# Attention and GRU on one core: four score banks shared with other stages, and a new order of every engine's turn

## The reference

```python
scale, shift = split(cond @ W_emb + b_emb)
xn = rms_norm(x, g_norm) * (1 + scale) + shift
q, k, v = heads(xn @ W_qkv)                  # q, k: rms_norm per head, times g_q, g_k
attn = softmax(q @ k^T * 16 ** -0.5)         # 32 x 32 per head
o = attn @ v
x = x + (o + o @ W_out)

gi = x_t @ W_ih + b_ih;  gh = h @ W_hh + b_hh         # for each of 32 time steps
r, z = sigmoid(i_r + h_r), sigmoid(i_z + h_z)
n = tanh(i_n + r * h_n)
h = (1 - z) * n + z * h                               # h starts as cond
out = x + all h
```

## Time and profile before

| what | us |
|---|---|
| median of three runs | 350.33 |
| the profiled execution | 349.93 |
| its span, from the first to the last instruction | 348.1 |
| PE busy (share of the span) | 331.1 (95%) |
| DVE busy | 246.8 (71%) |
| ACT busy | 237.1 (68%) |
| POOL busy | 224.5 (64%) |
| first input product of the first GRU step (L1233) | at 199.84 |

### The profile page before, as it was taken

How to read it: one execution, slowest core, us unless ns; L and a number is a source line. 1 busy time by engine, 2 the same in 40 slices (tenths; PEclk the granted TensorE clock), 3 DMA queues, 4 the chain that set the end, 5 groups by cost and what they waited for, 6 DMA issues and landing times.

```text
span 348.1 us, 14145 instructions
## 1 busy us (share of the span) xinstructions
PE 331.1 (95%) x5201; PEld 300.5 (86%) x5201; DVE 246.8 (71%) x664; ACT 237.1 (68%) x722; POOL 224.5 (64%) x404
## 2 busy tenths in 40 slices
PE   8989999999999999999998999999999999999994
PEld 8767888878788887878877899999999999999994
DVE  1779988898989889898889555555556555555555
ACT  4788777777777777777755756666666666666663
POOL 6788776676867677686858455555555555555552
PEclk9999999999999999999999999999999999999999
DMA  6961133622111211111111131111111121111111
GB/s 203 312 208 44 30 99 106 189 80 59 58 28 50 62 46 56 29 55 60 54 36 63 39 101 47 57 52 61 59 47 60 60 60 60 60 60 60 60 53 39
DMA packets 26576, 25.81 MB, mean 74 GB/s; under 512 B 3750, under 2 KB 25260, under 8 KB 26540
## 3 DMA queue, kind: packets, MB, share of 16 engines
q1 hardware_dynamic: 24828, 22.10, 20.7%
q10 hardware_dynamic: 1712, 3.21, 3.0%
HBM read 12.46 MB, written 8.39 MB: 60 GB/s over the span
## 4 chain that ended last, share of the span: by engine, by line
PE 87%; POOL 5%; issue 4%; DVE 2%; ACT 1%; POOLq 0%; ACTq 0%; DVEq 0%
PE bank L1233 37%; PE bank L1190 23%; PE bank L1353 8%; PE bank L1334 5%; PE bank L1370 5%; PE bank L1482 2%; PE bank L1317 2%; PE bank L1326 2%; PE bank L1196 2%; POOL wqkv_lo L554 1%; POOL oT_lo L502 1%; POOL xn L476 1%; POOL operands L465 1%; PE bank L1210 1%; POOL wih_lo L495 1%
## 5 line engine op out<-in xcount | busy, mean ns | idle before, releaser
L1233 PE MATMUL bank<-wih_lo,wo_parts 128*128 128x256 f32 x192 | 56.3, 294 | 0.0
L1233 PE MATMUL bank<-wih_hi,wo_parts 128*128 128x256 f32 x192 | 54.5, 285 | 0.2 <-POOL pair_lo L580 0.2
L1233 PE MATMUL bank<-wih_hi,pair_lo 128*128 128x256 f32 x192 | 52.7, 279 | 0.0
L1233 PE MATMUL bank<-wqkv_hi,hT_hi 128*128 128x256 f32 x192 | 52.6, 293 | 0.0
L591 POOL TENSOR_TENSOR operands<-operands,h 128x128 f32<-128x128 f32 x64 | 29.6, 462 | 34.0 <-ACT operands L880 33.2
L1233 PE MATMUL bank<-wqkv_lo,hT_hi 128*128 128x256 f32 x192 | 50.0, 279 | 0.0
L1190 PE MATMUL bank<-wqkv_hi,xn_hi 128*128 128x512 f32 (+1 forms) x124 | 46.5, 375 | 0.2 <-POOL xn_lo L511 0.2
L1133 DVE TENSOR_TENSOR operands<-bank,operands 128x128 f32<-128x128 f32 x64 | 18.6, 291 | 39.4 <-ACT operands L877 39.4
L1233 PE MATMUL bank<-wqkv_hi,hT_lo 128*128 128x256 f32 x192 | 42.7, 279 | 0.0
L598 POOL TENSOR_TENSOR w_emb_sb<-h,w_emb_sb 128x256 f32<-128x256 f32 x31 | 22.9, 737 | 30.7 <-DVE h L1150 30.7
L1190 PE MATMUL bank<-wqkv_lo,xn_hi 128*128 128x512 f32 (+1 forms) x124 | 41.9, 338 | 0.0
(11 more groups left out here) (137 smaller groups left out, 991.8 us busy)
## 6 DMA issues: line engine op xcount, KB each, us to landing
v_diag<-v_rows SPq DMA_DIRECT2D x128, 34.0 KB, 1.9
out_dram<-x SPq DMA_DIRECT2D x16, 256.0 KB, 2.2
w_emb_sb<-out_dram SPq DMA_DIRECT2D x32, 128.0 KB, 2.1
out_dram<-w_emb_sb SPq DMA_DIRECT2D x31, 128.0 KB, 1.7
x_in<-in_x_dram SPq DMA_DIRECT2D x7, 512.0 KB, 9.2
stage_w<-in_L_cond_W_ih_dram ACTq DMA_DIRECT2D x2, 384.0 KB, 3.4
w_hh_sb<-in_L_cond_W_hh_dram ACTq DMA_DIRECT2D x2, 384.0 KB, 3.4
w_emb_sb<-in_L_cond_W_emb_dram ACTq DMA_DIRECT2D x1, 512.0 KB, 4.3
```

Of the source, the lines that this page charges most:

```text
L1233: return pe.matmul(dst, moved, gate_columns(weights, k, block), start=False, stop=True, skip_group_check=True)
```

## The change

**Scores.** All 32 matmuls of a group follow one another without `s_half`; the four partition groups of the operands write to four banks, 0 to 3, of which each uses the first 128 columns. The head order of scores, maxima and PV follows.

**Other users of these banks.** PV goes to bank 0 from column 128, the input transposes to the right half of bank 2, OUT to the right half of bank 3. The new bank 4 has the result transposes and V, bank 5 QKT, banks 6 and 7 QK as before. Steps that share a bank now wait for each other: the scores for the last readers of PV, of input transposes and of OUT (`o_ready`, `xmod_ready`, `x2_ready`, the last for the OUT of the turn before), the input transposes and OUT for `logits_ready`, that is, until DVE has read the scores of the same turn, and the maxima for the PV of the same turn.

**Orders.** On PE the result transposes and V move from the turn's start to behind QKT (V only from turn 11 on; `early`). DVE takes the maxima and `logits` right behind `qkn`, and then `ss`, reciprocal, `o_sb`, residual, `xmod`, `probsT`, `oT`; from turn 34 on `qkn`, maxima, `logits`, `ss`, reciprocal, `o_sb`, `oT`, `probsT`, and last the residual. ACT begins with the copies of QKT and V, then the roots. POOL begins with the masked keys, then Newton, then shift. `LATE_RESULTS`, by which four result transposes and copies came at the end of a turn, is gone.

**Gate weights.** W_ih and W_hh lie side by side in `gate_stage` and are split in sixteen pieces (128 x 2 x 96 each), one in each looped turn: a cast on ACT, a subtraction on POOL. Their loads and those of the biases are issued by SP in turns 7 to 12 instead of by ACT in turns 11 to 15, and the bias sum is in turn 14 instead of 37. W_hh no longer takes W_qkv's place. The GRU's small tiles lie in `gate_stage`, the state products of the first step come in turns 39 and 41.

```diff
-PE_X2T, PE_V, PE_S, PE_PV, PE_QKT, PE_OUT, PE_XT, PE_QK = 11, 4, 7, 8, 5, 10, 2, 3
-DVE_QKN, DVE_SS, DVE_OT, DVE_MAX, DVE_RCP, DVE_XMOD, DVE_RES, DVE_O, DVE_PT = 4, 3, 8, 6, 7, 1, 9, 7, 6
+DVE_QKN, DVE_MAX, DVE_SS, DVE_RCP, DVE_RES, DVE_XMOD, DVE_PT, DVE_OT = 4, 6, 3, 7, 9, 1, 6, 7
-GATE_LOADS = 11
-LATE_RESULTS = range(24, 28)
-LAST_TURNS = range(34, 39)
+LAST_TURNS = NG + 2
...
-        p_xTw, p_vx2, p_qkT = (bank(f"bank{i}") for i in range(3))
-        p_s = ctx.enter_context(nc.psum_tensor("bank3", [P, 2 * BANK], F32))
-        p_o = bank("bank5")
+        p_s = ctx.enter_context(nc.psum_tensor("bank0", [P, 4 * BANK], F32))
+        p_vx2, p_qkT = bank("bank4"), bank("bank5")
+        p_o = p_s[:, P:P + GB * HEADS // 4 * VW]
+        p_xT = p_s[:, 2 * BANK + D:3 * BANK]
+        p_w = p_s[:, 3 * BANK + D:4 * BANK]
...
+            def gate_piece(n):
+                lo, whole, hi = (w[:, :, :].rearrange("p m (n f) -> p m n f", n=GATE_PIECES)[:, :, n, :]
+                                 for w in (gate_lo, gate_stage, gate_hi))
+                pool.wait_ge(gate_hi_ready, n + 1)
+                pool.tensor_tensor(lo, whole, hi.bitcast(F32), ALU.subtract).then_inc(gate_lo_ready, 1)
...
             def maxima(g, slot):
                 dve.wait_ge(s_ps, g + 1)
+                if later(g, 1):
+                    dve.wait_ge(o_ps, g)
...
@@ DVE body
+                last = isinstance(base, int) and base + u >= LAST_TURNS
...
+                if last and g is not None:
+                    probs_transposed(g, (u - DVE_PT) % 2)
...
                 o = group(base, u, DVE_RES)
                 if o is not None:
                     residual(o, (u - DVE_RES) % 4)
...
@@ input_transposes
+                if later(g, PE_S - PE_XT):
+                    pe.wait_ge(logits_ready, g - (PE_S - PE_XT - 1))
...
@@ scores
+                if later(g, 2):
+                    pe.wait_ge(o_ready, g - 1)
+                pe.wait_ge(xmod_ready, capped(g, PE_S - PE_XT))
+                if later(g, PE_OUT - PE_S + 1):
+                    pe.wait_ge(x2_ready, g - (PE_OUT - PE_S))
-                for n in range(2):
-                    if n == 1:
-                        pe.wait_ge(s_half, g + 1)
...
+                for c in range(KC):
+                    for b in range(GB):
+                        columns = slice(c * P + T * b, c * P + T * b + T)
+                        for j in range(NB):
+                            rows = slice(PB * j, PB * j + PB)
+                            dst = p_s[T * b:T * b + T, BANK * j + 2 * T * c:BANK * j + 2 * T * c + 2 * T]
...
@@ output_projection
-                pe.wait_ge(xmod_ready, capped(g, PE_OUT - PE_XT))
+                pe.wait_ge(logits_ready, capped(g, PE_OUT - PE_S + 1))
```

More of the change, by code:

```diff
@@ L411, in body @@
                     load_x(4 * FIRST_SPREAD, NG, x_loaded[FIRST_SPREAD])
+                for i in range(4):
+                    if turn_is(base, u, BIAS_LOADS + i // 2):
+                        load_bias(i)
+                    if turn_is(base, u, GATE_LOADS + i):
+                        load_gate_weights(i)
                 o = group(base, u, SP_X2)
@@ L526, in body @@
             def body(base, u):
+                k = group(base, u, POOL_KEYS)
+                if k is not None:
+                    mask_keys(k, (u - POOL_KEYS) % 2)
+                n = norm_item(base, u, POOL_NEWTON)
+                if n is not None:
+                    newton(n, (u - POOL_NEWTON) % 2)
                 g = group(base, u, POOL_XN)
@@ L540, in body @@
                     input_low_part(g, (u - POOL_XLO) % 2)
[L541 to L544, removed]
+                if turn_is(base, u, BIAS_SUM):
                     summed_biases()
[L546 to L555, removed]
+                if not isinstance(base, int):
+                    gate_piece(base + (u - FIRST_LOOPED))
             pool.memset(threes[:, :], 3.0).then_inc(threes_ready, 1)
@@ L664, in value_weights, with gate_piece @@
                 act.copy(wqkv_hi[:, :, 2 * D:3 * D], stage_w[:, :, 2 * D:3 * D]).then_inc(wv_hi_ready, 1)
[L666 to L691, removed]
+            def gate_piece(n):
+                hi, whole = (w[:, :, :].rearrange("p m (n f) -> p m n f", n=GATE_PIECES)[:, :, n, :]
+                             for w in (gate_hi, gate_stage))
+                act.copy(hi, whole).then_inc(gate_hi_ready, 1)
             def first_state():
@@ L794, in body @@
             def body(base, u):
+                if turn_is(base, u, FIRST_LOOPED - 1):
+                    for loaded in ih_loaded + hh_loaded:
+                        act.wait_ge(loaded, 16)
+                if turn_is(base, u, SET_GATES):
+                    act.wait_ge(bias_ready, 1)
+                    act.wait_ge(gates_clear[0], 1)
+                    set_gates(0)
+                g = group(base, u, ACT_QKT)
+                if g is not None:
+                    queries_keys(g, (u - ACT_QKT) % 2)
+                v = group(base, u, ACT_V)
+                if v is not None:
+                    values(v, (u - ACT_V) % 4)
                 n = norm_item(base, u, ACT_LN)
@@ L808, in body @@
                 d = group(base, u, ACT_X2T)
[L809 to L810 removed]
+                if d is not None:
                     result(d)
[L812 to L814 removed]
                 g = group(base, u, ACT_EXP)
@@ L817, in body @@
                     exponentials(g, (u - ACT_EXP) % 2)
-                for c in range(KC):
-                    if turn_is(base, u, NG + c):
-                        gate_weights(c)
+                if not isinstance(base, int):
+                    gate_piece(base + (u - FIRST_LOOPED))
                 n = group(base, u, ACT_SQX)
@@ L843, in body @@
                     second_squares()
-                for i in range(2 * KC):
-                    if turn_is(base, u, GATE_LOADS + i):
-                        load_gate_weights(i)
                 if turn_is(base, u, ACT_XN):
@@ L1088, in body @@
                     last_low_part((u - DVE_OT) % 2)
-                o = group(base, u, DVE_O)
-                if o is not None and not late_residual:
-                    attention_output(o, (u - DVE_O) % 2)
+                g = group(base, u, DVE_XMOD)
+                if g is not None:
+                    modulated(g, (u - DVE_XMOD) % 2)
                 g = group(base, u, DVE_PT)
-                if g is not None and not late_residual:
+                if g is not None and not last:
                     probs_transposed(g, (u - DVE_PT) % 2)
+                o = group(base, u, DVE_OT)
+                if o is not None and not last:
+                    attention_transposed(o, (u - DVE_OT) % 2)
                 if turn_is(base, u, 0):
@@ L1321, in result_transposes @@
                 pe.wait_ge(x2_ready, d + 1)
-                pe.wait_ge(v_ready, capped(d, PE_X2T - PE_V + (1 if isinstance(d, int) and d in LATE_RESULTS else 0)))
+                pe.wait_ge(v_ready, capped(d, PE_X2T - PE_V))
                 if later(d, 1):
@@ L1411, in body @@
                     query_key_transposes(g, (u - PE_QKT) % 2)
+                d = group(base, u, PE_X2T)
+                if d is not None:
+                    result_transposes(d, (u - PE_X2T) % 4)
+                if v is not None and not early:
+                    value_projection(v, (u - PE_V) % 2)
                 if turn_is(base, u, NG - 1 + PE_OUT):
```

173 lines of the change are left out of this document (69 added, 104 removed).

## The result

The changed kernel takes 368.19 us (median of four runs, 366.7 to 369.05) against 350.42 for the kernel before on the same chip: ratio 1.050, 95% interval 1.046 to 1.054. The forecast was 353.3, range 347.0 to 356.3. The sign was right and the size was not.

A forecast was written before the change was run, and what follows sets the result against it. PE was taken to set the pace, DVE 9% behind. Start +2.55, loop -6.3, tail +7.0 and GRU 0 summed to +3.2 on the profiled 349.93 us, giving 353.1 to 353.5; forecast 353.3, range 347.0 to 356.3.

The forecast's parts named there:

- The scores, 0.57: PE's merged 32 score matmuls take 0.57 us from their start to PV, where the two halves took 1.08.
- back to back: Rival for the scores: halves merely follow without the idle 0.24 and its restart, 0.64 us to PV, 355.5 us; chance 0.2.
- the sixteen tiles' 0.37: Rival: the array takes both score halves in the time of one, 0.37 us to PV, 347.5 us in all; chance 0.19.
- The new waits in the loop: Looped turns: maxima wait for PV and OUT for `logits`, a cycle of 5.27 us; -6.3 us over 23 turns.
- The start: Turns up to the fifth scores: +2.55 us, of which +1.55 from the first to the fifth scores through added waits.
- The +1.0 ahead of group 0: Before the first scores: POOL does masked keys ahead of the shift, so the input's low part comes later; +1.0 us.
- The tail: Scores of group 27 to the first GRU product: scores wait for DVE's residual, 35.4 against 28.43 us, +7.0.
- the clock to a rival: Rival: PE's holes in the tail halve its clock, some 5 us more, 358 us in all; chance 0.05.
- The pieces and the loads: Gate-weight pieces on ACT and POOL cost nothing in the loop; earlier weight and bias loads on SP's queue are hidden.
- The GRU: GRU steps behind the tail: same instructions with other names and banks, 0 us, both signs excluded.
- Merging gains nothing: Rival: scores stay 1.08 us because the four groups' matmuls follow at the old rate; +16, about 369 us; chance 0.03.

The follow-up runs named there:

- e1: Changed kernel with every score matmul of 64 columns cut into two of 32 columns, 64 matmuls instead of 32: 415.28 us, ratio 1.185.
- e10: Changed kernel with its 32 score matmuls of 64 columns issued twice over to the same places: 415.94 us, ratio 1.186.
- e2: Changed kernel with score matmuls reordered, the four column groups changing before the row groups: 369.05 us, ratio 1.053.
- e5: Changed kernel with two of a group's six QK products moved ahead of OUT from turn 11 on: 363.94 us, ratio 1.038.
- e6: Changed kernel with V behind QKT from turn 7 on instead of turn 11: 366.41 us, ratio 1.043.
- e3: Changed kernel with matmuls that nobody reads filling PE's idle times in turns 34 to 38: 365.49 us, ratio 1.042.
- e4: Kernel before with the gate-weight part of the change alone; banks, orders and scores untouched: 349.68 us, ratio 0.997.
- e9: Changed kernel, two QK products ahead of OUT, V late from turn 7; in the tail earlier residual, unread matmuls, OUT in bank 4: 359.49 us, ratio 1.025.

## Why the prediction was wrong

- **The scores, 0.57: this is the step that failed.** They took 0.82 on the mean. The price of 6.7 ns a record came from four records in 0.27 us, which are the first four of PV's 32 where the window of the rows ends; all 32 last 0.68. The rows of the halves said otherwise as well: 0.45 and 0.39 for 16 matmuls each, 0.84 without the idle 0.24. The bound "back to back" of 0.64 took off another 0.20 for a restart that no row shows; it should have been 0.84. Merging saved 0.26 us a turn, the idle 0.24 and little more. e1, e10 and e2 show that a matmul's price is by number, and neither columns nor order change it; the sixteen tiles' 0.37 did not come either. 0.25 in 32 turns is 8.0 us of the 14.9 by which the forecast missed. The Trainium skill, "TensorEngine Tiling (Array Packing)", section "Instruction Overhead", says that a matmul has some 60 cycles of overhead and that a narrow one takes as long as one of 60 columns. It was passed over for the rule on sixteen tiles: e1 and e10 agree with it in kind, with 20 ns a matmul.
- **The new waits in the loop: right.** PV to maxima to `logits` to OUT is the circle that sets the turn, and e5 shortens it. On the mean the maxima started 0.81 behind PV instead of 0.72, and OUT 0.79 behind `logits` instead of 0.74, which is the other 0.13 of the turn, or 3 us in 23 turns.
- **The start: the mechanism right in three gaps, one wait left out.** +3.3 for +1.55 from group 0 to 4. The first gap was 5.37 for 4.66: DVE's maxima stand behind `qkn`, which waits there for POOL's last Newton step; `qkn` starts at 27.13 and the maxima at 27.73, 1.35 behind the scores where the sum had 0.68. The other three were 5.61 for 5.27, by scores of 0.79 instead of 0.57 and the slower way round through DVE as in the loop. e6 takes 1.3 back. The +1.0 ahead of group 0 is not settled: it measured +1.4, but the first input landed 0.9 later in this execution, and over the experiments on the changed kernel group 0's scores start anywhere from 25.2 to 27.1.
- **The tail: right in its chain (7.0, and 8.3 with the true scores), wrong in leaving the clock to a rival.** The clock fell in the tail, and keeping PE busy in its idle times prices that at 3.2 us (e3). The forecast gave that 0.05, on rows in which no idle time was as long.
- **The pieces and the loads: right,** free in the loop (e4).
- **The GRU: 0 was forecast with both signs excluded; it measured -0.5,** and -0.6 in e4, which has only the gate weights' part of the change. Why is not shown.
- **"Merging gains nothing" gave 369** and so lies near the result, but for another reason than its own: merging did remove the idle 0.24, and the time went elsewhere.

## What to carry to other kernels

Price a run of small matmuls by the step from its start to the next stage's start, never by the few rows of a burst whose durations overlap; and take two lengths of run, since one length divided by its number (26 ns here) hides the fixed part that a second one shows (20 ns and 0.18 us). A PSUM bank that two stages share ties every reader of the one to every writer of the other: write the circle down through all engines and compare its sum with the sum of PE's own work. And where a change opens idle times in PE's work, look at the granted clock in and behind them before you price the tail.

## What the runs showed of the hardware that was not expected

A 32 x 32 f32 matmul with its weight load costs 20 ns in a run of them, with 32 columns as with 64 (1.46 and 1.48 us on the mean for 64 of them, 0.82 for 32), and the order in which the sixteen tiles are used does not change it (0.82). In an idle time of 2.82 us the granted clock fell from 1.00 to 0.50, and its mean from 190 to 200 us was 0.62; with 9.33 of these ten busy it stayed at 1.00. An idle time as long is not needed: in e9 the clock fell at 202.5 us, and no idle time of PE in its tail is longer than 1.66.
